# LSTM on one core: the input's share of the gates seeded by one pass over three stacked bf16 parts, in a loop over two rounds

## The reference, cut to what matters

```python
xW = jnp.einsum('ntd,dg->ntg', x, Wx) + b          # g = 4 * 512 gates
def step(carry, xw_t):
    prev_h, prev_c = carry
    a = xw_t + prev_h @ Wh
    i, f, o = sigmoid of a[:, 0:512], a[:, 512:1024], a[:, 1024:1536]
    g = jnp.tanh(a[:, 1536:])
    next_c = f * prev_c + i * g
    next_h = o * jnp.tanh(next_c)
```

## Time and profile before

| | |
|---|---|
| median of 3 runs | 8654.77 us (8653.25 to 8656.25) |
| span of the profiled execution, first to last instruction | 8652.0 us |
| PE busy | 7642.7 us (88%), 161068 matmuls |
| DVE busy | 6743.4 us (78%) |
| ACT busy | 3536.3 us (41%) |
| POOL busy | 569.1 us (7%) |
| instruction fetches in the whole run | queue q8: 20 packets, 0.33 MB; queue q14: 16 packets, 0.13 MB |

### The profile page before, as it was taken

One profiled execution on the slowest core, in us unless ns is written; L12 is line 12 of the kernel. 1 busy time (PEld: TensorE's weight loads), 2 busy tenths in 40 slices (PEclk: granted clock), 3 DMA queues, 4 the chain that ended last, 5 costly groups with the idle time before them and its releaser, 6 DMA issues. The chain is left out here.

```text
span 8652.0 us, 400132 instructions
## 1 busy us (share of the span) xinstructions
PE 7642.7 (88%) x161068; PEld 4218.0 (49%) x161068; DVE 6743.4 (78%) x44271; ACT 3536.3 (41%) x17511; POOL 569.1 (7%) x2117
## 2 busy tenths in 40 slices
PE   1899999999999999999984999999999999999998
PEld 1455555555555555555432555555555555555555
DVE  7777777777777777777677777777777777777777
ACT  4344444444444444444443444444444444444443
POOL 4000000000000000000011000000000000000000
PEclk5999999999999999999997999999999999999999
DMA  2000000000000000000001000000000000000001
GB/s 94 0 0 0 0 0 0 0 0 0 0 0 0 0 0 0 0 0 0 0 0 41 0 0 0 0 0 0 0 0 0 0 0 0 0 0 0 0 0 39
DMA packets 36420, 37.71 MB, mean 4 GB/s; under 512 B 10272, under 2 KB 26656, under 8 KB 36384
## 3 DMA queue, kind: packets, MB, share of 16 engines
q1 hardware_dynamic: 36384, 37.25, 1.3%
HBM read 28.85 MB, written 8.39 MB: 4 GB/s over the span
## 5 line engine op out<-in xcount | busy, mean ns | idle before, releaser
L371 PE MATMUL q_PA<-scratch,q_H 128*8 128x256 f16 x32768 | 1250.5, 273 | 39.2
L371 PE MATMUL p_PA<-scratch,p_H 128*8 128x256 f16 x32768 | 1251.2, 273 | 38.2
L371 PE MATMUL p_PB<-scratch,p_H 128*8 128x256 f16 x32768 | 1250.8, 273 | 0.0
L371 PE MATMUL q_PB<-scratch,q_H 128*8 128x256 f16 x32768 | 1250.2, 273 | 0.0
L555 DVE STREAM_TRANSPOSE p_GT<-p_PA 128x64 f32<-128x64 f32 (+1 forms) x3072 | 706.9, 255 | 506.3 <-PE p_PA L371 465.3
L555 DVE STREAM_TRANSPOSE q_GT<-q_PA 128x64 f32<-128x64 f32 (+1 forms) x3072 | 707.5, 255 | 504.9 <-PE q_PA L371 464.1
L371 PEld LDWEIGHTS p_PA<-scratch,p_H 128*8 128x8 f16 x32768 | 614.6, 85 | 587.2 <-DVE p_H L577 520.0
L371 PEld LDWEIGHTS q_PA<-scratch,q_H 128*8 128x8 f16 x32768 | 614.0, 85 | 588.1 <-DVE q_H L577 521.4
L371 PEld LDWEIGHTS p_PB<-scratch,p_H 128*8 128x8 f16 x32768 | 796.6, 87 | 98.7
L371 PEld LDWEIGHTS q_PB<-scratch,q_H 128*8 128x8 f16 x32768 | 796.0, 87 | 99.1
L365 PE MATMUL p_PA<-p_XP,p_SEL 128*128 128x256 bf16 x3075 | 512.5, 275 | 306.8 <-DVE p_GT L555 289.3
(11 more groups left out here) (181 smaller groups left out, 11583.5 us busy)
## 6 DMA issues: line engine op xcount, KB each, us to landing
scratch<-in_x_dram SPq DMA_DIRECT2D x8, 1024.0 KB, 5.3
out_dram<-xa SPq DMA_DIRECT2D x16, 512.0 KB, 5.9
xb<-in_L_cond_Wx_dram SPq DMA_DIRECT2D x8, 384.0 KB, 7.1
xb<-in_L_cond_Wh_dram SPq DMA_DIRECT2D x8, 384.0 KB, 7.2
xa<-in_L_cond_Wx_dram SPq DMA_DIRECT2D x8, 384.0 KB, 5.9
xa<-in_L_cond_Wh_dram SPq DMA_DIRECT2D x8, 384.0 KB, 5.9
xb<-in_L_cond_Wx_dram SPq DMA_DIRECT2D x8, 128.0 KB, 6.8
xb<-in_L_cond_Wh_dram SPq DMA_DIRECT2D x8, 128.0 KB, 7.1
```

What stands on the lines that cost most here:

```text
L371: last = nc.tensor.matmul(bank[Q * j:Q * j + 2 * B, 0:(hi - lo) * Q], H[:, u % 2, k, :], w16[:, part, k, j, lo * Q:hi * Q], start=False, s ...
```

## The change

- `seed` becomes four matmuls of 8 columns, one for each column tile, instead of three of 128. Their moving operand stacks the three bf16 parts of a round (32 rows each) and three rows with the parts of the bias in 99 partitions of `XP`, so that one pass adds all of it. They write only the 8 used rows of each tile; DVE clears the banks once.
- The parts are made without DVE. ACT copies `PX` to bf16 (`XS`, part 0, step 2 of a round), PE takes that part off the bank by multiplying it with minus the identity (`take_off`), ACT copies the rest (part 1, step 3), PE takes that off, ACT copies the last (part 2, step 4). Twelve DMAs a round on SP move the parts from `XS` into the stacked rows of `XP`.
- `PX` and `XC`, `XP`, `HH` are doubled, and the loop's body is now two rounds, `v` = 0 and 1, with 64 turns a layer. `TC` gives up its bank and becomes an SBUF tile of each group.
- `x_product` moves ahead of the wait for `tr_a`.
- The bias comes by 8 small DMAs; DVE splits it, and 24 DMAs put it into both buffers of `XP`. ACT waits for these (`biasp`) ahead of the first part.
- The semaphores of the steps are shared by the two layers.

```diff
-EARLY = 3
+AHEAD = U - 2
+PARTS = 3
+SEED_ROWS = PARTS * UB + PARTS
...
-        HH = sbt("HH", [P, U, NC * B])
-        XC = sbt("XC", [P, NC, UB])
-        XR = sbt("XR", [P, NG * Q])
-        bias = sbt("bias", [P, NG * Q])
-        XM = sbt("XM", [P, 2, NG * Q], BF16)
-        XP = sbt("XP", [P, 3, NG * Q], BF16)
-        SEL = sbt("SEL", [P, U, NJ, Q], BF16)
+        HH = sbt("HH", [P, 2, U, NC * B])
+        XC = sbt("XC", [P, 2, NC, UB])
+        XS = sbt("XS", [P, PARTS, NG * Q], BF16)
+        XP = sbt("XP", [P, 2, NJ, NG * Q], BF16)
+        SEL = sbt("SEL", [P, U, 2 * B], BF16)
+        NEG = sbt("NEG", [P, P], BF16)
...
-                self.tanh_c = TC[:, col:col + m]
+                self.tanh_c = sbt("TC" + name, [P, m])[:]
...
+            with sp.Fori(0, ROUNDS // 2) as r:
+                for v in range(2):
+                    now = sp.snap(r * 2 + (v + 2))
+                    sp.wait_ge(s["seeded"], now)
+                    for part, made in enumerate(("xhi", "xmid", "xlo")):
+                        sp.wait_ge(s[made], now)
+                        for j in range(NJ):
+                            sp.dma_start(XP[part * UB:(part + 1) * UB, 1 - v, j, :],
+                                         XS[Q * j:Q * (j + 1), part, :]).then_inc(s["xp"], 16)
...
+            def take_off(buf, part):
+                for j in range(NJ):
+                    last = nc.tensor.matmul(PX[buf][Q * j:Q * (j + 1), :], NEG[:, Q * j:Q * (j + 1)], XS[:, part, :],
+                                            start=False, stop=True, skip_group_check=True)
+                return last
+
+            def seed(u, buf, bank, lo, hi):
+                for j in range(NJ):
+                    last = nc.tensor.matmul(bank[Q * j:Q * j + 2 * B, 0:(hi - lo) * Q], SEL[0:SEED_ROWS, u, :],
+                                            XP[0:SEED_ROWS, buf, j, lo * Q:hi * Q], start=True, stop=False, skip_group_check=True)
+                return last
...
-            with pe.Fori(0, rounds) as r:
-                for u in range(U):
-                    now = pe.snap(r * U + (u + 1))
...
+            with pe.Fori(0, ROUNDS // 2) as r:
+                for v in range(2):
+                    for u in range(U):
+                        now = pe.snap(r * (2 * U) + (past + v * U + u + 1))
...
+                        buf = 1 - v if u < 2 else v
+                        if u == 2:
+                            pe.wait_ge(s["xc"], pe.snap(r * 2 + (v + 3)))
+                            pe.wait_ge(s["xlo"], pe.snap(r * 2 + (v + 1)))
+                        last = x_product(buf, (u + AHEAD) % U)
...
+                        if u == 2:
+                            pe.wait_ge(s["xhi"], pe.snap(r * 2 + (v + 2)))
+                            take_off(1 - v, 0).then_inc(s["sub"], 1)
...
-                    if u == U - 3:
-                        dve.wait_ge(s["xw"], r + 2)
-                        nc.vector.tensor_tensor(XR[:], PX[:], bias[:], ALU.add).then_inc(s["xr"], 1)
-                    if u == U - 2:
-                        rest_of_xr(r + 2)
-                    if u == U - 1:
-                        dve.wait_ge(s["seeded"], r + 1)
-                        last_part_of_xr(r + 2)
```

More of the change, by code:

```diff
@@ L53, in __getitem__ @@
         return self.h[n]
+STEP_SEMS = ("gates_a trg_a trif_a tr_a preg_a pre_a preo_a if_a ig_a c_a tc_a hi_a h_a "
+             "gates_b trif_b tr_b pre_b preo_b if_b ig_b c_b tc_b hi_b h_b")
 def in_chip_order():
@@ L314, in _ @@
                 load_weight(stage, wh, sp, s[f"wh{k}"], [k])
-            with nc.allow_non_contiguous_dma(reason="the bias of a column tile's units, on each of its rows"):
-                for j in range(NJ):
[L317 to L323, removed]
+            with nc.allow_non_contiguous_dma(reason="the bias in the order of the column tiles"):
+                v = b.rearrange("(g c j i) -> j g c i", g=4, j=NJ, i=Q)
+                for at, gates, units in in_chip_order():
+                    for g in range(gates.start, gates.stop):
+                        here = (at + (g - gates.start) * NF) * Q
+                        sp.dma_start(BF[:, here:here + NF * Q].rearrange("p (c i) -> p c i", c=NF),
+                                     v[:, g, units, :]).then_inc(s["bias"], 16)
@@ L340, in _ @@
[L340 to L351, removed]
+            with pool.Fori(0, ROUNDS // 2) as r:
+                for v in range(2):
+                    made = pool.snap(r * 2 + (v + 1))
+                    pool.wait_ge(s["xw"], made)
+                    for c in range(NC):
+                        last = nc.gpsimd.tensor_copy(XC[:, v, c, :], x_all[:, bass.ds(r * (2 * UB) + (c * XCOLS + (v + 2) * UB), UB)])
+                    last.then_inc(s["xc"], 1)
+                    ready = pool.snap(r * (2 * U) + (past + v * U + U + 1))
+                    pool.wait_ge(st["h_a"], ready)
+                    pool.wait_ge(st["h_b"], ready)
+                    for c in range(NC):
+                        here = xt[:, c, bass.ds(r * (2 * UB) + v * UB, UB)].rearrange("p (u b) -> p u b", b=B)
+                        last = nc.gpsimd.tensor_tensor(here, here, HH[:, v].rearrange("p u (c b) -> p u c b", b=B)[:, :, c, :], ALU.add)
+                    last.then_inc(s["xadd"], 1)
@@ L377, in _ @@
             for n in range(U):
-                last = x_product(n)
+                x_product(0, n)
             wh_arrived(pe)
@@ L387, in _ @@
             pe.wait_ge(s["sel"], 1)
[L388 to L394 removed]
+            pe.wait_ge(s["biasp"], 16 * PARTS * 2 * NJ)
+            pe.wait_ge(s["xp"], 16 * SEED_DMAS)
+            seed(0, 0, PA, 0, GA).then_inc(s["seeded"], 1)
+            seed(0, 0, PB, GA, NG).then_inc(s["seeded"], 1)
             first_half = [(k, part) for k in range(NF) for part in range(2)]
```

337 lines of the change are left out of this document (183 added, 154 removed).

## The result

| | before | changed |
|---|---|---|
| median | 8655.3 us (4 runs) | 9273.8 us (9264.8 to 9278.7, 4 runs) |
| ratio | | 1.0714, 95% interval 1.0698 to 1.0729 |
| span of the profiled execution | 8652.0 us | 9272.9 us |

The change makes the kernel 7.1% slower, 619 us. I had forecast 9050 with a range to 9260: the sign and the fetch at the return came out, the size is beyond the range's end. In all that follows, a median is that of the fast runs; single executions at a lower granted clock, or far above the others (up to 15373 us), are left out.

A forecast was written before the change was run, and what follows sets the result against it. The step's chain of handovers was taken to bound the kernel, with PE's instruction fetch at each loop return deciding the change: 8652 + 35 + 11 - 13 + 365 = 9050 us, range for 8 in 10 8680 to 9260.

The forecast's parts named there:

- What bounds a step: Each step is one handover after another between engines, 3.84 us a step; 2048 steps make 7864 of 8652 us.
- the zeros: DVE's removed operations, the new seeds, `x_product`, `take_off`, ACT's copies and SP's DMAs lie in slack: 0 each.
- `TC`: Tanh's output in SBUF lengthens each step's chain on ACT and DVE by 17 ns: +35 us, bounds 0 and 49.
- Ahead of the loops: Bias DMAs and later seeds before each layer's loop, less `x_product` done earlier: +11 us, bounds 0 and 20.
- The wait for POOL: DVE's 6.64 us wait in each layer's second round for POOL's first addition goes: -13 us.
- PE doesn't keep the new body: PE's loop body, 1196 to 2488 instructions, outgrows its store, so each branch back fetches; chance 0.76.
- The price of a return: At PE's branch back, a 3.3 us fetch with 0.4 hidden leaves 2.9 us, 126 times: +365 us.
- The clock: After PE's pause its clock may fall, +0.44 us a step; left out of the sum, up to 100 us in the range.
- the next blocks arrive while PE works, one packet in 1.7 steps: After a return, PE's later instruction packets come during its work; no cost was added for them.
- the pause is longer or brings a cold clock: Rival at PE's returns: 5.3 us a fetch, 4.9 exposed, gives 9300 us; within the fetching case's 0.76, no separate chance.
- DVE's miss would fall in the same pause: A similar instruction miss on DVE (356 instructions) at the return would lie within PE's pause; no cost added.

The follow-up runs named there:

- e3: Kernel before with only tanh's output `TC` moved from PSUM to an SBUF tile of each group: 8705.1 us, ratio 1.0056.
- e1: Kernel before with PE's loop body alone written out over two rounds, same instructions in the same order: 9304.4 us, ratio 1.0746.
- e6: Kernel before with PE's loop over two rounds and the low-part products of weight chunks 2 and 3 left out: 8847.6 us.
- e9: Kernel before with PE's loop over two rounds and the low-part products of weight chunks 1, 2 and 3 left out: 8630.2 us.
- e2: Kernel before with DVE's loop body alone written out over two rounds: 9077.6 us, ratio 1.0487.
- e11: Kernel before with PE's, DVE's and ACT's loops over two rounds and `TC` in SBUF: 9370.9 us, ratio 1.0822.
- e12: Changed kernel with 60 small matmuls ahead of the first layer's loop on PE, run a second time for its trace: 9246.6 us, one execution.
- e4: Kernel before with the loop bodies of PE, DVE and ACT over two rounds: 9322.5 us, ratio 1.0765.
- e10: Kernel before with PE's loop over two rounds and the low-part products of all four weight chunks left out: 8257.8 us.

## Why the prediction was wrong in its size

- **What bounds a step, and the zeros.** Right. An ordinary step grew by 24 ns, and e3 accounts for all of it. DVE lost 433 us of busy time (500 expected) and no step got shorter.
- **`TC`.** Right in sign and place, 35 us for 49: ACT's 16 of the 17 ns were not a matter of width, as e3's same eight columns show, and 10 was the wrong choice between the bounds. The sum of the upper bounds, 24 ns, was the value. The sentence of the Trainium skill cited for the sign (ScalarE: Activation LUTs) stands in the section Step-by-step: what each stage is for, not in the one named; e3's 162 and 178 ns are the comparison that 162 against 179 for sixteen columns could only suggest.
- **Ahead of the loops.** +11 expected, 15 measured. The seeds came at 227.03 us, as in this timeline of the changed kernel:

```profile
215.25 0.60 ACT L492 ACTIVATE p_XS<-p_PX 128x512 bf16<-128x512 f32 x1 [10.62 <-DMA p_XP<-p_XS]
...
224.19 2.74 DVE L601 SCALAR_TENSOR_TENSOR scratch<-xb,p_sc,scratch 128x512 f16<-128x512 f32 x4 [0.20 <-ACT scratch L498]
...
227.03 0.28 PE L408 MATMUL p_PA<-p_XP,p_SEL 99*8 99x256 bf16 x4 [2.59 <-DVE scratch L601]
```

  ACT waited for the bias DMA until 215.25, not 212; what stands behind that wait was counted rightly.
- **The wait for POOL.** -13 expected; the step that held it was 7.75 us longer than its neighbours before in the first layer and 7.23 in the second, and is now of ordinary length: -15. It didn't return a round later.
- **PE doesn't keep the new body.** Right, and the deciding step: 1543 packets, and e1 shows it without the rest of the change. The lengths were too small (1260 and 2618 rows, not 1196 and 2488), so ten packets were too few; that changed no side. The Trainium skill's 2048 instructions for PE (Runtime: NRT & Kernel Launch, Instruction fetch mechanics) gave the right side here, but e6's 2006 rows don't stay and e9's 1750 only at some returns, so the measurement puts the limit lower. Its rule that a taken branch to a missing page waits for it agrees with the record of 3.5 us.
- **The price of a return: the step that failed.** I had "2.9 us remain": a fetch of 3.3, 0.4 hidden. The fetch was 3.5 (3.71 in this branch's record, less the 0.2 of a branch that is kept), and 0.4 us of it hidden, near enough: PE resumes at 2288.93, `h_b`'s turn would have been at 2286.45 (0.05 after DVE's end), and with 0.65 us of products still to do that is 3.13 late. But from 2288.93 to the transposes at 2291.03 it took 2.10 us, where 0.65 + 0.71 = 1.36 was the count at full clock: 0.74 more, together 3.87 for the 3.85 measured. The next step lost another 0.64, to the second stop and to what remained of the half clock. In the sum: 3.1 + 0.74 + 0.64 = 4.5 instead of 2.9, x 126 = 567 instead of 365. So the 202 us that are missing in the forecast's term are mostly not the fetch but what follows it.
- **What was left out of the sum.** Two terms. The clock: I had the row for it, worked out 0.44 us of a step, and put it in the range only. The slow matmuls stand behind the pauses of e2, e11 and e12 too, and ten groups of matmuls lie between a return and the gates of `PA`, not four, so it belonged into the sum. And "the next blocks arrive while PE works, one packet in 1.7 steps": the second packet starts only when PE has resumed and does not arrive in time, so PE stands a second time, in the median 0.4 to 0.7 us in the changed kernel's layers and 1.1 to 1.6 in the second layers of e1 and e11. The rival "the pause is longer or brings a cold clock" named half of this, but its 9300 came from 5.3 us for the fetch, which is not what happened; that it lies close to 9274 is luck.
- **DVE's miss would fall in the same pause.** Right for this kernel (e4: 18 us), and by itself worth 422 us, which I hadn't priced.

A return of the same body costs different times in two layouts: 4.5 us in the changed kernel, 4.9 and 5.4 in e1's two layers, 4.6 and 6.05 in e11's. That this comes in part from where the second packet begins is shown by e12, in both layers. How the rest divides between the stops and the clock, and what decides at which returns e9 misses in its first layer, stays open.

## What to carry to other kernels

Count the instructions of a loop's body for each engine before unrolling it by two, and look in the profile's instruction queues for packets inside the loop: none means that it is kept, a number that grows with the turns means a pause at each return. Count in the trace, between two branches, since an operation of the program can be more than one row there. Price such a return by more than the fetch: the pause, the products behind it at half clock, and the stop at the next packet. Where alternating buffers can be written without doubling the body, that is worth trying (no run here does it), and when two engines' bodies both outgrow their stores, mending one of them shows less than its worth, since the pauses lie side by side.

## What the runs showed of the hardware

- PE kept a loop body of 1494 rows (e10) and didn't keep 2006 (e6); 1750 rows (e9) were kept at 40 of 63 returns of one layer and at none of the other. A body that isn't kept is fetched whole in each turn, in packets of 16 KB and some 256 rows: 9, 10, 11 and 12 a turn for 1750, 2006, 2262 and 2518 rows.
- At a return that misses, the packet starts 1.0 us after the branch, takes 1.0 us and PE resumes 1.5 us after its end (medians of the changed kernel). The next packet starts 0.6 us after that, and PE stops at its first instruction if it gets there earlier.
- DVE keeps 183 instructions and doesn't keep 364 (e2), with packets of 8 KB on q14, five a turn; the pause is 3 us too.
- After 2.5 to 4 us without a matmul PE's clock was granted in full for a moment and then near its lower level, though PE was busy: 0.55 over 3.8 us in the changed kernel, 0.50 over 6 us in e11.
- ACT writes eight columns into SBUF in 178 ns (e3) and into PSUM in 162, input in PSUM both times.
